# Twelve yt buffers, the last group's odds on GpSimd, the first expert tile turned in the last attention step, early table loads

## What is computed

```python
# attention: 16 heads of 8 channels, window 32, 16 global tokens
x = x + tanh(g_xattn) * attention(layernorm(x), ctx, ctx, mask)
# experts: 8, top 2 per token, 128 -> 512 -> 128
h = layernorm(x)
w, idx = top_k(softmax(h @ gate_w), 2);  w = w / w.sum(-1)
for i in range(8):
    wi = where(idx == i, w, 0).sum(-1)
    out += (silu(h @ w1[i]) * (h @ w3[i])) @ w2[i] * wi
x = x + tanh(g_ffn) * out
```

## Time and profile before

| | us |
|---|---|
| median of 3 runs | 459.47 (458.91 to 459.83) |
| span of the profiled execution | 458.1 |
| TensorE busy | 407.4 (89%) |
| VectorE busy | 290.9 (64%) |
| GpSimd busy | 259.4 (57%) |
| ScalarE busy | 239.6 (52%) |
| TensorE busy in the stretch 242 to 259 | 17.0 of 17 |
| in 259 to 266 | 4.77 of 7 |
| in 266 to 290 | 24.0 of 24 |
| in 290 to 316 | 23.0 of 26 |
| in 316 to 442 | 126 of 126 |

### The profile page before, as it was taken

One profiled execution on the slowest core, in us unless ns is written; L12 is line 12 of the kernel. 1 busy time (PEld: TensorE's weight loads), 2 busy tenths in 40 slices (PEclk: granted clock), 3 DMA queues, 4 the chain that ended last, 5 costly groups with the idle time before them and its releaser, 6 DMA issues.

```text
span 458.1 us, 14422 instructions
## 1 busy us (share of the span) xinstructions
PE 407.4 (89%) x4547; PEld 360.1 (79%) x4548; DVE 290.9 (64%) x786; ACT 239.6 (52%) x564; POOL 259.4 (57%) x312
## 2 busy tenths in 40 slices
PE   2879979999999998997879899988999999999970
PEld 1647658877777776776669799888999999999960
DVE  3876798887888887889546368544444554554420
ACT  2758506667677675766666534233444444444430
POOL 5743554334654737473646568776666665655560
PEclk9989979999999999999999999999999999999995
DMA  7964557457766666485223233334444343333235
GB/s 215 279 123 94 96 96 185 90 105 113 170 147 136 152 134 161 106 216 169 65 69 75 45 52 48 54 67 61 69 70 58 44 54 46 46 47 40 24 29 189
DMA packets 74783, 46.24 MB, mean 101 GB/s; under 512 B 8608, under 2 KB 71490, under 8 KB 74562
## 3 DMA queue, kind: packets, MB, share of 16 engines
q1 hardware_dynamic: 59072, 34.84, 33.2%
q0 software_dynamic: 12272, 8.92, 14.9%
q10 hardware_dynamic: 3392, 1.88, 1.7%
HBM read 18.12 MB, written 14.20 MB: 71 GB/s over the span
## 4 chain that ended last, share of the span: by engine, by line
PE 62%; DMA 9%; issue 7%; DVE 6%; ACT 6%; POOL 4%; ACTq 2%; POOLq 1%; DVEq 0%
PE ps_scores L1612 20%; PE ps_max_scores L1620 10%; DMA sums_scratch<-yt,xg 8%; PE ps_values L897 7%; PE ps_max_scores L853 6%; PE ps_scores L883 5%; PE ps_scores L837 3%; PE ps_max_scores L837 2%; POOL expert_rows_scratch L1328 2%; PE ps_out L921 1%; ACT xn L474 1%; DVE rsplit L1119 1%; ACT w_all L464 1%; DVE qkf L558 1%; POOL sums_scratch L1733 1%
## 5 line engine op out<-in xcount | busy, mean ns | idle before, releaser
L1733 POOL DMA_INDIRECT sums_scratch<-yt,xg x71 | 115.9, 1633 | 66.9 <-DMA sums_scratch<-yt,xg 28.1
L1612 PE MATMUL ps_scores<-xgT,qs 128*128 128x128 f32 x1136 | 141.1, 278 | 5.1 <-ACT xgT L1658 3.8
L1612 PEld LDWEIGHTS ps_scores<-xgT,qs 128*128 128x128 f32 x1136 | 134.1, 194 | 7.1 <-ACT xgT L1658 4.5
L1699 DVE TENSOR_TENSOR qs<-qs,ps_scores 128x512 f32<-128x512 f32 x71 | 48.8, 688 | 88.4 <-PE ps_scores L1612 70.5
L1119 DVE TENSOR_REDUCE rsplit<-ps_max_scores 128x4 f32<-128x512 f32 x128 | 84.8, 685 | 15.0 <-PE ps_max_scores L837 11.2
L1328 POOL DMA_INDIRECT expert_rows_scratch<-xr,pos x64 | 66.4, 1037 | 25.6 <-issue 13.1
L1620 PE MATMUL ps_max_scores<-w_all,qs 128*128 x568 | 75.6, 276 | 2.8 <-ACT yt L1669 2.3
L1620 PEld LDWEIGHTS ps_max_scores<-w_all,qs 128*128 128x128 f32 x568 | 69.0, 192 | 3.8 <-issue 3.6
L1027 ACT ACTIVATE pT<-ps_scores 128x1024 f32<-128x1024 f32 x64 | 62.0, 1022 | 18.1 <-PE ps_scores L837 17.8
L1662 ACT ACTIVATE qs<-ps_scores 128x512 f32<-128x512 f32 x71 | 42.3, 596 | 30.3 <-PE ps_scores L1612 30.3
L1669 ACT ACTIVATE yt<-ps_max_scores,xg 128x128 f32<-128x128 f32 x71 | 26.1, 368 | 60.4 <-PE ps_max_scores L1620 40.4
(11 more groups left out here) (202 smaller groups left out, 527.8 us busy)
## 6 DMA issues: line engine op xcount, KB each, us to landing
qs<-w_all SPq DMA_DIRECT2D x96, 64.0 KB
ks<-w_all SPq DMA_DIRECT2D x96, 64.0 KB
w_all<-in_L_ffn_w_dram SPq DMA_DIRECT2D x24, 256.0 KB
xg<-expert_rows_scratch SPq DMA_DIRECT2D x71, 65.0 KB, 1.9
xs<-in_x_dram SPq DMA_DIRECT2D x4, 512.0 KB, 5.6
sums_scratch<-xs SPq DMA_DIRECT2D x8, 256.0 KB, 4.5
sums_scratch<-yt,xg POOLq DMA_INDIRECT x71, 3.3
expert_rows_scratch<-fill SPq DMA_DIRECT2D x16, 65.0 KB, 2.5
```

The lines of the kernel that those rows point to most:

```text
L1612: ins = nc.tensor.matmul(bank[u % 2][:, c * P:(c + 1) * P], w13[:, u % 2, n, c * P:(c + 1) * P], xgT[:], start=True, stop=True)
L1699: nc.vector.tensor_tensor(hidT[:, u % 2], act_s[:, u % 2], ps_b[u % 2], ALU.mult).then_inc(hid_ready, 1)
L1733: pool.indirect_dma_start(out=z_d, out_offset=bass.IndirectOffsetOnAxis(ap=xg_u[:, u, X_IDX:X_IDX + 1], axis=0), in_=yt[:, u % YRING], in_ ...
```

## The change

It does five things. (1) `yt` has twelve buffers instead of four; they lie in the memory of `va`, the values of attention, and the old place stays reserved. The four `sent` semaphores stay; scale_out(t) waits for send(t - 12) instead of send(t - 4), and send(t) on GpSimd waits for send(t - 4). (2) The last group's odds are no longer an Exp on ScalarE at t = 7 with an addition and a reciprocal on VectorE at t = 8, but e to the power of the gap, plus one, to the power of -1, on GpSimd at t = 10. (3) Turning tile 0 and copying it go into the last step of attention (batch 31); VectorE's copy of tile 0's weights goes ahead of normalise(30), that of tile 1's stays behind it; the first steps of the experts are put in another order. (4) In that hand-over ScalarE's square(29), norm_rows and copy_choice of the group before the last go from the last step of attention behind copy_rows(1), and the last squares go to late(1) and late(2). (5) Two small activations load tables early: Sqrt behind ScalarE's first three DMA issues, Silu right behind attention's last step.

```diff
-    YRING = 4
+    SENDS = 4
@@
-        yt = sb("yt", [P, YRING, D])
+        sb("rest_of_early", [P, SENDS, D])
@@
+        yt = va[:].rearrange("p b h w -> p (b h w)")[:, 0:RING * D].rearrange("p (u d) -> p u d", d=D)
@@ project_gpsimd
+            pool.memset(warm[:, 0:1], 1.0).then_inc(warm_ready, 1)
             pool.memset(ident[:], 0.0).then_inc(pool_step, 1)
...
+            pool.memset(euler[:], float(np.e))
+            pool.memset(minus_one[:], -1.0)
@@
+        def load_table(act, function):
+            act.wait_ge(warm_ready, 1)
+            nc.scalar.activation(warm[:, 1:2], warm[:, 0:1], function)
+
         def project_scalar(act):
             for n, src in (("q", wq), ("k", wk), ("v", wv)):
                 act.dma_start(w_sb[n][:], src).then_inc(proj_loaded, 16)
+            load_table(act, ACT.Sqrt)
@@ attend_tensor, after
-                elif part == 2:
+                elif part == 1:
                     turn_attn(AFTER.plus(-1))
-                elif part == 3:
+                else:
                     project(AFTER.plus(-1))
@@ attend_tensor, step
                     turn_max(at.plus(2))
+                if at.known and at.b == B - 1:
+                    turn_rows(pe, 0, 0, 0)
                 if at.exists():
                     values(at, 0)
@@ attend_scalar, step
+                if at.known and at.b == B - 1:
+                    copy_rows(act, 0)
+                    copy_attn(last)
+                    return
@@ attend_scalar, after and late
                 if part == 0:
+                    load_table(act, ACT.Silu)
                     copy_values(AFTER.plus(-1))
-                    square(AFTER.plus(-2))
+                elif part == 1:
+                    norm_rows(route(AFTER.plus(-1), 3), 1)
+                    copy_choice(route(AFTER.plus(-1), 3))
                 else:
                     copy_attn(AFTER.plus(-1))
...
                 if t == 1:
+                    square(AFTER.plus(-3))
+                    square(AFTER.plus(-2))
+                elif t == 2:
                     square(AFTER.plus(-1))
...
-                elif t == 7:
-                    odds(LAST)
@@ attend_vector, step
-                if out:
-                    normalise(out)
                 if at.known and at.b == B - 1:
                     for loaded in w_loaded:
                         dve.wait_ge(loaded, 16 * 3 * E // WEIGHTS)
                     dve.wait_ge(scored, (B - GB) * NB)
-                    for t in range(2):
-                        copy_weights(dve, t, t)
+                    copy_weights(dve, 0, 0)
+                if out:
+                    normalise(out)
+                if at.known and at.b == B - 1:
+                    copy_weights(dve, 1, 1)
@@ attend_vector, late
+                if t == 2:
+                    dve.wait_ge(res_done, B)
...
-                    for part in range(3):
+                    for part in range(2):
                         places(LAST, part)
@@ attend_gpsimd
+            def last_odds():
+                pool.wait_ge(gap_ready, NG)
+                pool.tensor_tensor(ed[:], euler[:], ed[:], ALU.pow).then_inc(last_step, 1)
+                pool.wait_ge(last_step, 1)
+                pool.tensor_scalar(ed1[:], ed[:], 1.0, 0.0, ALU.add, ALU.add).then_inc(last_step, 1)
+                pool.wait_ge(last_step, 2)
+                pool.tensor_tensor(ed1[:], ed1[:], minus_one[:], ALU.pow).then_inc(last_step, 1)
+                pool.wait_ge(last_step, 3)
+
             def place_rows(r):
-                pool.wait_ge(place_step, r.g * 4 + 4)
+                pool.wait_ge(place_step, r.g * 4 + (2 if r is LAST else 4))
...
                     if n == 0:
+                        last_odds()
                         place_rows(LAST)
@@ experts_tensor
-            turn_rows(0, 0, 0)
             up(0, 0)
+            turn_rows(pe, 1, 1, 0)
             after(0)
-            turn_rows(1, 1, 0)
+            up(1, 1)
             after(1)
-            up(1, 1)
+            turn_rows(pe, 2, 2, 0)
+            down(0, 0, expert(pe, 0))
             after(2)
-            turn_rows(2, 2, 0)
-            down(0, 0, expert(pe, 0))
-            after(3)
@@ experts_scalar
-                if not (isinstance(t, int) and t < YRING):
-                    act.wait_ge(sent[u % YRING], sent_before(u, turn) * 16)
-                nc.scalar.activation(yt[:, u % YRING], ps_d, ACT.Copy, scale=xg[:, u, X_GATE:X_GATE + 1])\
+                if not (isinstance(t, int) and t < RING):
+                    act.wait_ge(sent[u % SENDS], sent_before(u, turn - 1) * 16 + 16)
+                nc.scalar.activation(yt[:, u], ps_d, ACT.Copy, scale=xg[:, u, X_GATE:X_GATE + 1])\
...
-            copy_rows(0)
             after(0)
-            copy_rows(1)
             gate(0, 0)
+            copy_rows(act, 1)
             after(1)
-            late(0)
-            for t in range(1, LATE):
+            gate(1, 1)
+            after(2)
+            copy_rows(act, 2)
+            scale_out(0, 0, 0)
+            late(1)
+            for t in range(2, LATE):
                 step(t, t % RING, t // RING)
                 late(t)
@@ experts_gpsimd, send
+                if not (isinstance(t, int) and t < SENDS):
+                    pool.wait_ge(sent[u % SENDS], sent_before(u, turn) * 16)
```

More of the change, by code:

```diff
@@ L1526, in build @@
         yt_ready = sem("yt_ready")
-        sent = [sem(f"sent{u}") for u in range(YRING)]
+        sent = [sem(f"sent{u}") for u in range(SENDS)]
         out_stored = sem("out_stored")
@@ L1554, in sent_before @@
         def sent_before(u, turn):
-            return turn * (RING // YRING) + u // YRING
+            return turn * (RING // SENDS) + u // SENDS
         def copy_weights(dve, t, u):
```

39 lines of the change are left out of this document (22 added, 17 removed).

## The result

The kernel after takes **468.57 us** (median of 4 runs, 466.21 to 470.47), the kernel before 459.65 (4 runs, 458.91 to 463.33): a ratio of **1.0173**, interval 1.0113 to 1.0233. I had said 456.4, in a range up to 460.6. The profiled execution of after has a span of 468.8 us, 10.7 more than before; it is one of the two longer ones of the four (470.46 us; the others took 466.21, 466.68 and 470.47).

The account below looks back on a forecast made before the run. TensorE was taken as the bound, with GpSimd's sends and SyncE's loads allowing 8.1 us gain at tile 33. Span: 458.1 - 1.1 (start) - 3.7 (experts) + 1.7 (clock) = 455.0; with 1.4 around it 456.4 us, range 453.4 to 460.6.

Parts of the forecast that it names:

- The start: Projections: early Sqrt table load runs beside ScalarE's DMA issues, square root near 8.0 instead of 9.18; -1.1 us.
- Rival one: Start: ScalarE's queue stands still during the table load, later DMAs delayed; +0.7 for -1.1, so 458.2 us; chance 0.18.
- The hand-over: Attention's end to first expert tiles: TensorE 1.9 us earlier, GpSimd's first send 1.05 us later.
- The odds by power: GpSimd at tile 10: two powers and an addition delay sends by 3.2 us (2.8 to 6.6); TensorE gains 4.1.
- rival three: GpSimd at tile 10: VectorE's work stretches the powers to 6.6 us or more; slower, 462.0 us; chance 0.10.
- the term of 4.1 us: TensorE, D(1) to D(17): gain credited to removing the table loads around tile 8.
- The output buffers: Experts: with twelve yt buffers ScalarE no longer waits for sends; TensorE's lost 5.4 us go away.
- The stop at tile 33: TensorE stands 7.7 us for tile 33's load, behind SyncE's 12.0 us of fixed work; then 1.7 us clock loss.
- The slack: GpSimd and SyncE at tile 33: 8.1 us, so TensorE can gain no more than that there.
- the 3.7 that I left as gain: Experts at D(32): what remains of TensorE's 11.4 us gain after the stop at tile 33.
- Rival two: Experts: no stop at tile 33, so all 11.4 us stay; 447.0 us; chance 0.06.
- the 11.4 that I had counted: TensorE up to D(32) without anything late: 1.9 from hand-over, 4.1 from odds, 5.4 from buffers.

Follow-up runs that it names:

- e5: The kernel after, unchanged, run again on another chip: 496.41 us, ratio 1.0216 to the kernel before.
- e6: The kernel after with 416 unused bytes ahead of xs, so all behind stands 512 bytes further than before: 485.53 us, ratio 0.9982.
- f3: The kernel before with 96 unused bytes ahead of qs alone, moving qs, ks and pT: 492.88 us, ratio 1.0183.
- e2: The kernel before with an unused buffer of 96 bytes ahead of xs, nothing else: 462.88 us, ratio 1.0030.
- e9: The kernel after with xs and va moved to 512 bytes, but qs, ks and pT 96 further: 490.41 us, ratio 1.0102.
- f4: The kernel before moved by 256 bytes from the token rows on: ratio 0.9996.
- e10: The kernel after with xs and va left at 96, but qs, ks and pT at 512: 486.87 us, ratio 1.0008 to the kernel before.
- e7: The kernel before with everything from xs on moved by 512 bytes, nothing else: ratio 1.0045.
- e1: The kernel after with an unused buffer of 32 bytes ahead of xs, 128 in all: 462.54 us, ratio 1.0022 to the kernel before.
- e3: The kernel before with an unused buffer of 64 bytes ahead of xs: ratio 1.0098.
- f5: The kernel before with w_all moved by 96 bytes to a multiple of 256, and everything from the token rows on by 512: ratio 0.9998.
- e4: The kernel before with the early Sqrt load alone, its buffer behind all others so nothing moves: ratio 0.9966.
- e12: The kernel after with all at 512 and the last group's odds back on ScalarE and VectorE: 480.35 us, ratio 0.9866 to the kernel before.
- f2: The kernel after at 512, odds back on ScalarE and VectorE, four output buffers instead of twelve: ratio 1.0053 to the kernel before.
- f1: The kernel after at 512, odds back on ScalarE and VectorE, tail stores between the loads of tiles 24 to 31: ratio 0.9853 to the kernel before.
- e11: The kernel after with all at 512 and SyncE's eight tail stores one by one behind loads 24 to 31: ratio 0.9965 to the kernel before.
- f6: The kernel after at 512, odds back, tail stores between loads, w_all also moved by 96 bytes: 451.18 us, ratio 0.9809 to the kernel before.

## Why the prediction was wrong, point by point

**The step that failed** is one that I did not take: "The new buffers lie in va, which nothing reads any more", and with it twelve buffers were done. I had asked for each edit which instructions it adds, and for the three small buffers the answer was a memset or two. I didn't ask what lies behind them in memory; the sum has no term for it, so it stands there at nothing, without a reason. They moved qs and ks by 96 bytes, and attention was 10.3 us longer in the two profiles. That the place does this in the kernel after is shown by e5 against e6 (496.4 and 485.5 us, 9.9 of the difference in attention). On the kernel before f3 shows its direction (+1.8%, +1.2% by the medians). None of my rivals had it; even the slower one ended at 462.0.

How large the price is stays open. The time that the queue's packets take grows by 9 to 10 us in e2, f3 and e9, with nothing or little else changed, and by 14.8 in after and 13.7 in e5 (against e6); but attention in the profiled executions grew by 2.5 in e2 (162.1 for 159.6), 1.4 in f3 (against f4) and 2.0 in e9 (against e10), and by 10.3 and 9.9 in after and e5. So a bad place of qs and ks is part of the loss wherever it was tried; that it makes all of the 10 us by itself is not shown. What the rest of the change adds to it, or xs at 96 together with qs at 96, or the chip, no run separates.

The Trainium skill has a rule close to this one: "DMA: Bandwidth & Descriptors", section "How a descriptor splits into AXI transactions", says that a descriptor is split into transactions that start at multiples of 256 bytes; one that doesn't begin there is read from the boundary below, and the bytes ahead of it still cost. Worked out from it, a piece of 512 bytes needs three transactions at 96, 64 or 128 past such a multiple and two at 256 or 512. For the destination the runs fit this: the queue's packets take 162.7 to 164.5 us with moves by 256 and 512 (f4, e6, e7) and 171.5 to 176.6 with qs and ks at 96 (e9, f3, e5), and on the other chip 151.9 against 160.1 to 162.1 (e1 to e3). They don't fit for the source, which is what the page speaks of: w_all had been off a multiple of 256 all along, and putting it on one gave 0.9998 (f5).

**The start** was right. The queue issues beside the load (2.35 while the load runs from 2.27), the square root came 1.06 earlier in e4, and the ratio 0.9966 is 1.6 us; -1.1 was said. In after itself it was hidden by token rows that landed 0.6 later, and after's first exps came 1.0 later, not 1.1 earlier. Rival one, a queue that stands still for the load, is fallen.

**The hand-over** was right to within 0.15 us: up(0) 0.74 earlier (said 0.87), up(2) 1.87 (1.86), the first send 0.98 later (1.05).

**The odds by power** were right as to their own length: 2.8 to 6.6 and +3.2 were said, 3.23 measured. But they delayed the sends by less, as the small operation behind them no longer took 1.69: from send 10 to send 11 it is 7.85 us where before it was 6.25, so 1.6 more, and send 20 is at last 3.25 later than before, with 4.25 said; 2.3 of it come behind the first send. On one chip, e10 with the powers and e12 without, the same step is 8.24 and 5.28 and send 20 comes at 91.4 and 87.8 behind the exps of batch 31. The two powers took 1.46 and 1.35 against the 1.04 of the earlier trace rows; far from 6.6 in all, so rival three is fallen too. The rule of the Trainium skill on shared SBUF interfaces ("GPSIMD Engine Reference", section "Key points"), which I set beside it, may be in these 0.3 to 0.4 us each, but no run separates it. On TensorE the term of 4.1 us was **mis-sized**. The table loads stayed in e12 and the step to D(8) was 4.30, only 1.5 over 2.79; in f2, with four buffers, it was 6.41. About 2.1 of what I gave to the odds belongs to the buffers (the same step lies between 5.27 and 6.91 in the kernel before and its moves, so 1.0 to 2.6). So the powers bought 1.5 us of TensorE at tile 8, where it was about to lose them at tile 33 anyhow, and paid with 2.3 us (after) to 3.6 us (e10 against e12) on the chain of sends that sets tile 33. e12 shows the balance on its own chip: 0.9866 without them, 1.0008 with them (e10).

**The output buffers** did what was said. ScalarE's waits for sends fell from 19.9 us in ten to this:
```profile
ACT va L1709 <- DMA sums_scratch<-va,xg: 1.5, 2, 0.9
```
Their worth depends on what is next. f2 against e12: D(32) 4.6 us later with four, the stage 234.1 for 229.4 (two chips); f2 against f1, on one chip: 8.1 us, which holds the tails' move too.

**The stop at tile 33** was the number on which I rested the forecast, and it was there, released by the load that I named, behind 11.9 us of SyncE's fixed work (12.0 said; 330.53 to 342.43), and a clock loss behind it. But its place was wrong by one tile. I wrote that TensorE turns tile 33 "right before D(32) = 338.10"; it does so before D(31) = 335.31. The slack was 5.3 us, not 8.1, and so 2.8 us of the 3.7 that I left as gain were never there. The turn of tile 33 and D(31), before:
```profile
335.20 0.27 PE L1604 MATMUL ps_values<-ident,xg 128*128 128x128 f32 x1
335.31 1.06 PE L1620 MATMUL ps_max_scores<-w_all,qs 128*128 x8
```
The load of tile 33 came 3.06 later against attention's end (342.43 - 239.45 for 328.08 - 228.16), less than the 4.25 that I said, which left 2.2; the slow products behind the stop then took 1.95 of it (4.74 us from D(31) to D(32) for 2.79), so D(32) was 0.1 earlier, and with 0.5 behind the last down product the stage gained its 0.6. Without the placement after would have been at about 459, as e6 (0.9982) says for its chip: "same", not faster. So even beside the large miss, the sum was 2.8 us too good by that step.

**Rival two**, no stop at all, is what e11, f1 and f6 built. D(32) came 9.4 us earlier in f6, with the odds on ScalarE; of the 11.4 that I had counted 4.1 were for the odds. Its end was not 447.0 but 451.2, since GpSimd's sends then set the end.

## What to carry to other kernels

Before an edit is costed at nothing because it only adds a small buffer, see what lies behind that buffer: here the destination of many transfers of 512 bytes did best at a multiple of 256. Tiny buffers can go to the end of memory, as in e4, or be padded out, as in e6. When a wait is removed, walk the step that comes next in program order, not in tile order, to find which tile is needed when; an error of one tile was here three quarters of the gain. And work moved off an engine that waits onto the chain that others wait for can be a loss even where its own length is priced correctly: two removed table loads saved TensorE 1.5 us at tile 8 and cost the chain of sends 2.3 to 3.6, and the version without the powers was the faster one (e12 against e10).

## What the runs showed of the hardware that was not expected

- Placement of a destination: the same 59072 packets took 162.7 us of the DMA engines with qs and ks at a multiple of 256 bytes, 171.9 with them 96 off (f4, f3), and the kernel was 1.8% slower (1.2% by the medians). The source's place did nothing (0.9998).
- ScalarE's queue issues DMAs while the engine loads a table: issue at 2.35, load from 2.27 to 3.55.
- The same kernel takes 460 us on some chips and 486 on others, with attention 160 and 186 us long and the rest of the kernel before within 1 to 2 us. With qs and ks 96 off, the kernel before lost 0.3% on one of the former (e2) and 1.8% on one of the latter (f3), the kernel after 1.7% and 2.2% (after, e5). Why is open.
- A small operation on GpSimd took 1.69 us at tile 10 in the kernel before, beginning 0.4 us ahead of the end of a send's row, and 0.27 in after, beginning 3.4 us behind it. The first power took 1.46 in after and 2.16 in e10, where it began 0.5 us ahead of such an end. What stretches them is open.
- After a stop of 6.22 us TensorE's products took 3.00 us for 1.95, until 349.3; over 344 to 351 the granted clock was 0.68 of full speed:
```profile
344.00:351.00 7.00, 6.72 (x42) 6.70 (x43) 1.38 (x2) 1.87 (x5) 5.58 (x4) 0.68 0.49 75
```
